# Third cross attention: key halves of the exponentials added by GpSimd and VectorE, row totals from half as many products, one unit later

## The reference

```python
qn = _l2norm(qh, axis=-2)            # 8 batches, 8 heads of 16 rows, 256 columns
kn = _l2norm(kh, axis=-2)
qk = ALPHA * jnp.einsum('bhdq,bhdk->bhqk', qn, kn)
sm = jax.nn.softmax(qk, axis=-1)
out = jnp.einsum('bhqk,bhdk->bhdq', sm, vh)
...
x = x + jnp.tanh(g_xattn[2]) * _L2_xattn_ref(_layernorm(x, axis=-1), ctx_2048, ctx_2048)
```

## Time and profile before

| what | us |
|---|---|
| median of 3 runs | 801.65 |
| lowest and highest | 798.29, 808.28 |
| the profiled execution, its own time | 804.65 |
| its span in the profile | 802.7 |
| TensorE matmul busy | 712.9 (89%) |
| VectorE busy | 535.0 (67%) |
| ScalarE busy | 393.2 (49%) |
| GpSimd busy | 361.8 (45%) |
| mean granted TensorE clock | 0.967 of full |

### The profile page before, as it was taken

One profiled execution on the slowest core, in us unless ns is written; L12 is line 12 of the kernel. 1 busy time (PEld: TensorE's weight loads), 2 busy tenths in 40 slices (PEclk: granted clock), 3 DMA queues, 4 the chain that ended last, 5 costly groups with the idle time before them and its releaser, 6 DMA issues.

```text
span 802.7 us, 13936 instructions
## 1 busy us (share of the span) xinstructions
PE 712.9 (89%) x4709; PEld 399.6 (50%) x4709; DVE 535.0 (67%) x1203; ACT 393.2 (49%) x714; POOL 361.8 (45%) x407
## 2 busy tenths in 40 slices
PE   6989889999997877878889898999999999999883
PEld 4444456444652322323336454555579858686431
DVE  4869975476769998999998967655411244026764
ACT  3568724211047988988993546662113343412211
POOL 3423123252414777788885612111610077942435
PEclk9999998999999998999999999999999999979997
DMA  9700002027209999999994004507741235961022
GB/s 272 173 7 1 2 24 76 0 23 146 42 1 163 166 195 175 186 184 193 182 186 87 1 1 125 155 2 191 176 145 47 81 123 133 289 156 53 1 21 33
DMA packets 227108, 84.66 MB, mean 105 GB/s; under 512 B 188863, under 2 KB 225095, under 8 KB 227047
## 3 DMA queue, kind: packets, MB, share of 16 engines
q1 hardware_dynamic: 224102, 78.62, 46.0%
q0 software_dynamic: 2944, 5.25, 2.7%
HBM read 33.50 MB, written 8.40 MB: 52 GB/s over the span
## 4 chain that ended last, share of the span: by engine, by line
PE 50%; DVE 16%; DMA 11%; issue 10%; POOL 8%; ACT 3%; SPq 2%; POOLq 0%; DVEq 0%; ACTq 0%
DMA hT<-hT 6%; POOL hT L1497 5%; PE psum L1020 5%; PE psum L991 4%; PE psum L2095 4%; DVE psum L1562 3%; DMA xn<-hT 3%; PE psum L1687 3%; DVE cx L2723 2%; PE psum L2374 2%; DVE am L903 2%; PE psum L497 2%; PE psum L1939 2%; PE psum L1956 2%; PE psum L666 2%
## 5 line engine op out<-in xcount | busy, mean ns | idle before, releaser
L1562 DVE TENSOR_SCALAR_CACHE_REDUCE psum<-psum,arena 128x1024 f32<-128x1024 f32 x128 | 158.7, 1285 | 9.9 <-PE psum L1384 9.2
L361 POOL TENSOR_TENSOR rstd<-ve,neg_half 128x1 f32<-128x1 f32 x64 | 39.9, 627 | 161.5 <-DVE ve L351 160.7
L1384 PE MATMUL psum<-arena 128*128 128x512 bf16 x256 | 81.3, 401 | 35.4 <-ACT arena L1468 23.3
L1497 POOL TENSOR_SCALAR hT<-arena 128x1024 f16<-128x1024 f32 x86 | 89.8, 1044 | 41.8 <-ACT arena L1468 23.0
L1468 ACT ACTIVATE arena<-psum,am 128x1024 f32<-128x1024 f32 x86 | 95.8, 1114 | 14.5 <-POOL hT L1497 7.0
L1384 PEld LDWEIGHTS psum<-arena 128*128 (+1 forms) x256 | 15.5, 98 | 70.9 <-issue 32.8
L1497 POOL TENSOR_SCALAR hT<-sg 128x1024 f16<-128x1024 f32 x42 | 43.9, 1044 | 11.3 <-ACT sg L1468 3.5
L1468 ACT ACTIVATE sg<-psum,am 128x1024 f32<-128x1024 f32 x42 | 46.8, 1114 | 4.1 <-DVE psum L1562 2.4
L1372 PE MATMUL psum<-hT,arena 128*32 128x256 f16 x352 | 42.7, 282 | 1.1 <-DMA hT<-hT 0.5
L2233 POOL DMA_INDIRECT arena<-moe_out,route x16 | 15.8, 990 | 58.4 <-DMA moe_out<-arena 54.4
L2438 POOL TENSOR_TENSOR hT<-hT,weights 128x512 f16<-128x512 f32 x32 | 39.4, 1272 | 0.9 <-DMA hT<-in_L_ffn_expert_masks 0.9
(11 more groups left out here) (466 smaller groups left out, 1658.1 us busy)
## 6 DMA issues: line engine op xcount, KB each, us to landing
hT<-in_L_ffn_expert_masks SPq DMA_DIRECT2D x32, 256.0 KB, 3.5
arena<-in_L_ffn_w_gate SPq DMA_DIRECT2D x2, 1408.0 KB
arena<-in_L_ffn_w_up SPq DMA_DIRECT2D x2, 1408.0 KB
arena<-in_L_ffn_w_down SPq DMA_DIRECT2D x2, 1408.0 KB
moe_in<-xT SPq DMA_DIRECT2D x2, 1024.0 KB, 8.9
hT<-moe_in SPq DMA_DIRECT2D x4, 512.0 KB, 5.0
moe_out<-arena SPq DMA_DIRECT2D x16, 128.0 KB, 1.7
hT<-hT SPq DMA_TRANSPOSE x83, 3.3
```

The costliest lines, as they stand in the source:

```text
L361: pool.tensor_tensor(rstd[:, t:t + 1], ve[:, t:t + 1], neg_half[:, t:t + 1], ALU.pow).then_inc(sig("ln_rstd"), 1)
L1384: mm = pe.matmul(psum[:, score_banks(c), :][:, g, :], QT[:, bass.ds(row_tile(j, c), 1), pair, :].rearrange("p t q -> p (t q)"), KT[c % 2][ ...
L1497: pool.tensor_scalar(Y1[:, n % Y_SLOTS, :], pe1(n), 255.0, 1024.0, ALU.mult, ALU.add)\
L1562: dve.tensor_scalar(s, s, size1[:, bass.ds(n, 1)], None, ALU.mult, ALU.min, accum_out=am[:, bass.ds(n, 1)])\
```

## The change

Instead of multiplying both key halves of the exponentials by ones, the two halves are added first, elementwise (`sum2`, 128 x 512 float32, into `PS2`, a free part of `hT` with 4 slots), and the block of ones multiplies the sum: 4 products a unit where there were 8. Of four pairs, GpSimd adds three and VectorE the fourth (p % 4 == 3). The totals of unit u come after the value products of unit u + 1 (`totals`). `v2_done` now counts totals; a new `v2_values` counts value products. The exponential of pair p now waits for value products and for the sum that read its slot. VectorE's sum stands first in `add(b)`, ahead of the wait for the batch's totals. GpSimd's masked keys and `rstd_pool` are spread between its sums, in units 3 to 6 and from unit 6 on.

Apart from that, `biases_loaded` is merged into `small0_loaded` (each waiter now waits for all 12 loads), `mask4_ready` into `bq0_scaled`, and `acc3_zeroed` into `consts3`.

```diff
-            dve.wait_ge(sig("biases_loaded"), 16 * len(BIAS_ROWS))
+            dve.wait_ge(sig("small0_loaded"), 16 * (4 + len(BIAS_ROWS)))
...
-            act.wait_ge(sig("small0_loaded"), 64)
+            act.wait_ge(sig("small0_loaded"), 16 * (4 + len(BIAS_ROWS)))
...
+        PS2 = hT[:, 0:2, :].rearrange("p a n -> p (a n)").rearrange("p (s g q) -> p s g q", s=SLOTS2, g=2)
+
+        def by_vector(p):
+            return p % 4 == 3
+
+        def wait_sums2(eng, n):
+
+            eng.wait_ge(sig("sums2_by_pool"), n - n // 4)
+            if n // 4:
+                eng.wait_ge(sig("sums2_by_dve"), n // 4)
+
+        def sum2(eng, p):
+
+            u = p // 2
+            eng.wait_ge(sig("p2_ready"), p + 1)
+            if u >= 2:
+                eng.wait_ge(sig("v2_done"), 4 * (u - 1))
+            x = PT2[:, p % SLOTS2, :, :, :]
+            eng.tensor_tensor(PS2[:, p % SLOTS2, :, :], x[:, :, 0, :], x[:, :, 1, :], ALU.add)\
+               .then_inc(sig("sums2_by_dve" if by_vector(p) else "sums2_by_pool"), 1)
...
-                        pe.matmul(out[32 * g:32 * g + 32, :], VP[:, kc, b, 2 * g + k, :], p,
-                                  start=first, stop=last, skip_group_check=True)
-                    for g in range(4):
-                        p = PT2[:, (2 * u + g // 2) % SLOTS2, g % 2, kc, :]
-                        mm = pe.matmul(total[32 * g:32 * g + 32, :], ones2[:, k, :], p,
-                                       start=False, stop=last, skip_group_check=True)
+                        mm = pe.matmul(out[32 * g:32 * g + 32, :], VP[:, kc, b, 2 * g + k, :], p,
+                                       start=first, stop=last, skip_group_check=True)
                         if kc == DC - 1:
-                            mm.then_inc(sig("v2_done"), 1)
+                            mm.then_inc(sig("v2_values"), 1)
+
+            def totals(u):
+                b, k = divmod(u, 2)
+                total = out2_bank(b)[1]
+                wait_sums2(pe, 2 * u + 2)
+                for g in range(4):
+                    pe.matmul(total[32 * g:32 * g + 32, :], ones2[:, k, :], PS2[:, (2 * u + g // 2) % SLOTS2, g % 2, :],
+                              start=False, stop=k == 1, skip_group_check=True).then_inc(sig("v2_done"), 1)
...
+                if u >= 2:
+                    totals(u - 2)
+            totals(STEPS2 - 1)
...
-                    act.wait_ge(sig("v2_done"), 4 * (u - 1))
+                    act.wait_ge(sig("v2_values"), 4 * (u - 1))
+                    wait_sums2(act, p - 3)
...
             pool.wait_ge(sig("q2_spread"), 2)
-            for b in range(NB // 2, NB):
-                masked_keys(pool, b)
-            for b in range(NB):
+            for p in range(2 * STEPS2):
+                if not by_vector(p):
+                    sum2(pool, p)
+                if p % 2:
+                    u = p // 2
+                    if 3 <= u < 3 + NB // 2:
+                        masked_keys(pool, u - 3 + NB // 2)
+                    if u >= 6 and u % 2 == 0:
+                        rstd_pool(pool, 5, u // 2 - 3)
+            for b in range(STEPS2 // 2 - 3, NB):
                 rstd_pool(pool, 5, b)
...
                 share = inv2[:, b, :]
+                sum2(dve, 4 * b + 3)
                 dve.wait_ge(sig("v2_done"), 8 * (b + 1))
...
-            dve.wait_ge(sig("acc3_zeroed"), 1)
+            dve.wait_ge(sig("consts3"), N_CONSTS3)
```

More of the change, by code:

```diff
@@ L844, in xa0_pool @@
         def xa0_pool(pool):
-            pool.wait_ge(sig("small0_loaded"), 64)
+            pool.wait_ge(sig("small0_loaded"), 16 * (4 + len(BIAS_ROWS)))
             pool.tensor_scalar(bq0, bq0, HD ** -0.5, None, ALU.mult).then_inc(sig("bq0_scaled"), 1)
@@ L848, in xa0_pool @@
             pool.wait_ge(sig("xq_ready"), NB)
-            pool.tensor_tensor(mask4, mask8[:, 0:4], mask8[:, 4:8], ALU.add).then_inc(sig("mask4_ready"), 1)
-            pool.wait_ge(sig("mask4_ready"), 1)
+            pool.tensor_tensor(mask4, mask8[:, 0:4], mask8[:, 4:8], ALU.add).then_inc(sig("bq0_scaled"), 1)
+            pool.wait_ge(sig("bq0_scaled"), 2)
             for b in range(NB):
@@ L2724, in ff3_dve @@
                     step(r) if k == 0 else ring_v.release(r)
-        N_CONSTS3 = 6
+        N_CONSTS3 = 7
         def consts3_pool(pool):
@@ L2730, in consts3_pool @@
             pool.wait_ge(sig("km_ready"), NB)
-            pool.memset(acc3, 0.0).then_inc(sig("acc3_zeroed"), 1)
+            pool.memset(acc3, 0.0).then_inc(done, 1)
             exact = dict(allow_small_or_imprecise_dtypes=True)
             pool.iota(places, pattern=[[P, NB]], base=0, channel_multiplier=1, **exact).then_inc(done, 1)
-            pool.wait_ge(done, 1)
+            pool.wait_ge(done, 2)
             pool.tensor_copy(meta.bitcast(I32)[:, :, 0], places).then_inc(done, 1)
@@ L2778, in loads0 @@
                 load(sp, bias_left[32 * k:32 * k + 32, h * D:(h + 1) * D],
-                     (own[bias] if bias in own else A[bias]).partition_broadcast(32), "biases_loaded")
+                     (own[bias] if bias in own else A[bias]).partition_broadcast(32), "small0_loaded")
             load(sp, gates_raw[:, 0:4], A["g_xattn"].partition_broadcast(P), "small0_loaded")
```

## The result

| | median, us | lowest to highest | runs |
|---|---|---|---|
| before, beside it | 802.58 | 798.29 to 808.28 | 4 |
| changed | 816.62 | 809.25 to 819.44 | 4 |

The ratio is 1.0141, 95% interval 1.0086 to 1.0197: the changed kernel is slower, by less than 2%, but by more than the range allowed for (up to 811). The profiled execution took 815.31 us with a span of 813.6.

What follows compares the result with a forecast made beforehand. TensorE bounds the third cross attention. First reciprocal at 504.3 plus turns 5.0 + 5.5 + 5 x 5.9 gives 544.3 against 542.17, +2.1 us: 806.8 for the profiled execution, 803.8 on the median; range 797.5 to 811.

Steps and rivals of the forecast that it cites:

- TensorE bounds the stage before, and all behind it moves one for one: Third cross attention: TensorE never idle, 2.94 us a unit; a shift of the last reciprocal shifts the program equally.
- The removed 0.43 us a unit: TensorE, third cross attention: one of four product groups goes, 2.94 to 2.51 us a unit, 6.9 us over 16 units.
- The price of a GpSimd sum: GpSimd's 128 x 512 float32 tensor_tensor in the third cross attention: 1.00 us from start to start.
- The start of the stage: First units of the third cross attention: TensorE waits 1.2 us for two GpSimd sums, losing its head start; first reciprocal 504.3.
- The loop without waits: VectorE's loop, totals through reciprocal, add, norm and sum to totals: 4.94 us a batch, against TensorE's 5.00.
- The delays: VectorE instructions waiting for GpSimd ones in each batch's loop: 0.95 us a turn, making it 5.9 us.
- The sum of the turns: Seven turns from first to last reciprocal: 5.0 + 5.5 + 5 x 5.9, ending at 544.3 instead of 542.17.
- The bias wait: Program start: VectorE's bias split waits 0.8 us longer, hidden by 2 us of cover before TensorE's product at 20.49.
- The other merges: Merged constants cost nothing, VectorE having waited already; ScalarE's new wait for sums is met long before the slot is wanted.
- The clock: Rival, chance 0.1: TensorE's granted clock falls inside the stage, each fall costing up to 1.7 us; 806.
- the turn goes well over 5.88 us: Rival, chance 0.25: `xn` and VectorE's sum meet GpSimd's back-to-back sums; turn 6.8, +6.6 us, 808.3.

Runs made afterwards that it cites:

- the three comparisons pooled: The unedited changed kernel against the kernel before, measured three times: ratios 1.0141, 1.0017 and 1.008, weighted together 1.0076, about 6.1 us.
- experiment 8: Changed kernel, but GpSimd waits for the transposes before its first masked key instead of its first sum: 814.95 us, one execution.
- experiment 2: Changed kernel, but the bias rows have their own semaphore again: 810.47 us, ratio 1.0134 to the kernel before.
- experiment 4: Changed kernel, but GpSimd adds the first key half to itself: 818.11 us in one execution, turn 6.18, stage 54.42.
- 7: Changed kernel, but VectorE's sum for the next batch stands right behind the reciprocal: 805.47 us, ratio 1.0045 to the kernel before.
- experiment 6: Changed kernel, but VectorE's sums add only 4 of 256 columns: 813.20 us, one execution, turn 6.12.

## Why the prediction was wrong

It said no change to speak of (+2.1 us), and it was slower. In its own terms the +2.1 were 1.05 at the start (the first reciprocal at 504.3 for 503.25), 1.08 in the turns (40.0 us for 38.92) and nothing for the bias wait; measured were 2.4, 3.7 and 0.8. The mechanism that it named was right. The steps that failed are the price of GpSimd's sum, the size of the delays in a turn, and the cover of the bias wait. Step by step:

- **TensorE bounds the stage before, and all behind it moves one for one.** Held as far as the profiles reach, to the router's softmax (13.59 and 13.60 us behind the last reciprocal). To the end of the program it isn't shown by itself; the pooled 6.1 us agree with it. The removed 0.43 us a unit was right as well: a unit with nothing idle takes 2.51 us (experiment 8).
- **The price of a GpSimd sum: failed.** "A 128 x 512 float32 tensor_tensor of GpSimd costs 1.00 us", from the earlier trace rows. It costs 1.23 (1.28 as recorded). The row was of a product of two broadcast inputs; that of a product with two full inputs, 1.27, stood in the earlier trace rows, and was put aside because its output is half as wide. Experiment 4 shows that the inputs decide: the same instruction is down to 1.04 once it reads one input twice.
- **The start of the stage: right in kind, too small.** TensorE does wait for two GpSimd sums, 1.69 us instead of 1.2. What I left out is the next wait: the first batch's totals need VectorE's sum as well, which met a GpSimd sum and took 1.77 us, 0.58 of it seen by TensorE. The first reciprocal came 16.00 us after the first scores, against 14.66: 1.34 us of the miss. "The head start is lost completely" held. Two reasons were worth about the same, each with the clock's fall in the same place: GpSimd's late start 0.9 us (experiment 8 beside 7) and the price of the sums 0.9 (experiment 4 beside 7, 13.43 for 14.29).
- **The loop without waits: nearly right.** 4.94 worked out, 5.08 measured.
- **The delays: mechanism right, size wrong.** I took 0.95 us a turn, "half a product, 0.5 us, on average", over four instructions. Measured: `xn` 0.49 and the sum 1.06, 1.55 together, and none in the add and the variance. It isn't an average. The turn locks: GpSimd's two sums start 0.3 us behind the totals (533.85 and 534.17, the idle time before them put down to L1986), VectorE's instructions hang on the totals half a turn earlier, so each turn meets the same sums at the same point, and three turns on end were alike (6.64 to 6.66). "Unequal starts make a full wait each time unlikely" was the wrong sentence; starts are equal. With 1.00 for GpSimd's sum the same phase gives 0.26 + 0.83 = 1.09 (experiment 4), close to the 0.95. So of the 0.75 us by which a turn was missed, 0.47 are the wrong price again (6.65 for 6.18), 0.14 the loop without waits, and 0.14 the average. That 0.95 would have been nearly right at the price assumed is in part luck, since it was made of four waits and only two occur.
- **The sum of the turns** was 40.0 us and came to 42.62. The turns 3 to 6 are 0.75 to 1.2 longer than 5.9. The longest, 7.13, is the first with an `xn` in it, and that `xn` waits for 0.96 (it takes 1.36). In that turn GpSimd makes its last masked keys (519.17), a power, and three sums without a pause until 525.07. The other three masked keys lie in the first two turns, which took 5.37 and 5.10 for the predicted 5.0 and 5.5. The prediction had no term for masked keys; what they cost is not shown by itself. The last turn, 5.07, is short: GpSimd has no sum left to make beside its `xn` and its sum (0.40 and 0.68).
- **The bias wait: failed.** "2 us of cover" was read from L667, which does start at 20.49. The wait for the split (line 658) stands ahead of both L666 and L667, so the products that start at 18.60 wait for it too. The trace had put the 0.83 us before it down to "issue", and I didn't look for the wait in the code. TensorE's product came 0.7 us later on average, 0.8 in the first pair of profiles (experiment 2). That the whole program ends as much later is likely, but too little for the times to show.
- **The other merges** cost nothing that shows. ScalarE's new wait for sums isn't empty, as the prediction had it: in each turn of 6.65 one exponential stands 1.31 us for VectorE's sum. It adds nothing that shows, as TensorE waits for the same sum.
- **The clock.** The grant did fall once more in the changed kernel, behind the last totals, which had stood 2.5 us for a sum:

```profile
546.00:549.00 3.00, 0.62 (x12) 0.13 (x4) 2.93 (x8) 0.00 (x0) 0.86 (x2) 1.00 0.00 0
549.00:554.00 5.00, 4.85 (x26) 2.92 (x27) 3.83 (x10) 1.39 (x3) 0.77 (x2) 0.66 0.06 5
```

  TensorE was busy for 0.62 of 3 us, and in the next stretch the granted clock is 0.66, a mix with the level of 1.2 GHz. It lies beside VectorE's last batch, and nothing of it reaches the chain up to the router's softmax (13.60 us, as above). The rival's place for it, inside the loop with TensorE standing 1.4 us a turn, didn't happen.

The rival "the turn goes well over 5.88 us" was the true case in each of its words, with 6.8 for the turn and 6.65 measured: the place (`xn` and the sum behind it), the two back-to-back sums, the price of 1.27. It gave +6.6 us; with the 0.8 of the bias wait it is +7.4, where the timelines have 6.9, the three comparisons pooled 6.1, and the first alone 14. I gave it 0.25 and should have given it the most, since of the two rows for the price one had the inputs of the new instruction and the other hadn't. The range failed on a further count: one comparison of so few runs can lie 5 to 8 us beside the difference of the kernels, and I had left 3 for it.

The Trainium skill, page "SBUF — State Buffer", section "Who interferes with whom", says that a VectorE instruction with two SBUF inputs contends with a GpSimd one that reads SBUF, and that whoever issues first has the shared ports for the whole instruction. Experiment 6 agrees in the sharpest form: 8 elements a row wait 1.07 us. The Trainium skill's page "GPSIMD Engine Reference", section 3.1, gives a tensor_tensor of GpSimd about 2.6 cycles an element and counts cycles at 1.2 GHz; for 512 elements an estimate by it is 1.1 us ahead of any fixed cost. The 1.23 us here agree, and it would have spoken against 1.00.

## What to carry to other kernels

Before new work is put into an engine's queue, write down the loop that it closes: here sum, totals, reciprocal, next batch, sum. The cure was one place in the queue: the sum right behind the instruction at whose time its inputs are ready took 6.2 us off the turns of the stage, where the removal of nearly all of VectorE's new work took 3.2 off (experiment 6). Take the price of a new instruction from a row with the same kinds of inputs, two full ones or one, and find the point of the turn at which each VectorE instruction meets a GpSimd one: here the waits were the same in each turn (0.49 and 1.06 us), not an average. Before two starts or stages are compared, see that the low clock lies in the same place in both: it was worth 1.7 us here, and made the gain of one edit look like 2.6 for 0.9. And where a profile calls the idle time before an instruction "issue", read the lines ahead of it in the code for a semaphore.

## What the runs showed of the hardware that I had not expected

- A GpSimd tensor_tensor of 128 x 512 float32 takes 1.23 us from start to start with two different inputs, 1.00 with one input read twice or with two broadcast inputs.
- VectorE waits for the whole GpSimd instruction however small its own is: 0.16 us became 1.23.
- Of one kernel the single run lies anywhere within about 12 us of its median, along the mean granted clock of TensorE (about 5.8 us for 0.01), while every turn of the stage repeats to 0.02 us. The timelines settled here what the times couldn't.
